# Gated delta rule: values and outputs turned in 32x32 blocks on VectorE and by transfers, gate projection token-major, another order

## The chip, the cores and the metric

One core of one Trainium2 chip runs the whole program in one launch. The metric is device time in microseconds (us) of that core, the median of several runs. The engines are TensorE (PE in the profile; PEld is its weight load), VectorE (DVE), ScalarE (ACT), GpSimd (POOL) and SyncE (SP), which here only issues transfers.

## The reference

One decoder layer in fp32 over x of 4 x 512 tokens of width 512: x plus a gated delta rule on the layernormed x, plus a retention-like cross attention with a context, plus a feed-forward with ternary weights. The change is in the first part. There are 16 key heads and 32 value heads of 128:

```
mixed = silu(causal_conv1d(h @ w_qkv, conv_w))      # taps of 4 tokens, per channel
q, k  = l2norm(q), l2norm(k);  v = v                # 16, 16 and 32 heads
beta  = sigmoid(h @ w_b);  g = -exp(A_log) * softplus(h @ w_a + dt_bias)
for each token t:                                   # per value head, state S is 128 x 128
    S = S * exp(g_t)
    S = S + k_t (x) ((v_t - k_t S) * beta_t)
    o_t = q_t S / sqrt(128)
core = o * rsqrt(mean(o^2) + eps) * norm_weight * silu(h @ w_z)
x1   = x + core @ w_out
```

## The kernel before

`head` layernorms x into xT (channels on partitions), and makes the decay tables. `delta_rule` then runs 64 units: 16 groups of heads (one key head with its two value heads) times 4 batches of 512 tokens, the batches of a group one after the other. A unit's 512 tokens are 4 chunks of 128, and within a chunk the recurrence becomes products with the inverse of a triangular matrix, found by doubling in 6 levels. `tail` does the projection with w_out and the rest of the layer.

Each engine has its own stream, written out by hand as a list of calls in one `slot` function, and the streams meet only in semaphores. A slot works on several units at once. Before the change there are three roles: `project` (unit n), `invert` (unit m = n-1) and `recur` (unit s = n-2), and `slots` runs 66 of them. The helper `long_slots`, with a fourth role `finish` (unit f = n-3) and 67 slots, is there but not used.

Names that matter, for a unit:

- `tile(n, j)` on TensorE projects one 128-wide tile over 512 tokens: k, q, v0, v1 and the gates z0, z1 (j = 0 to 5), each 4 products of 128x512 in fp32, which show as 8 instructions (L646). Each goes to one of three PSUM banks of a ring, whose order and release are written down in `RING_ORDER`, `RING_BANK` and `RING_FREED`.
- `first_tap` (ScalarE, L1116) copies a tile scaled by the last conv tap, `convolve` (VectorE, L937) adds three more, `silu` (ScalarE) finishes. The conv taps of a group lie in the last columns of `wc`, one buffer; `first_tap(n, 0)` waits for them (`taps_loaded`) in a group's first unit. SyncE reloads them after the last tap of the group's last unit, and before the change it does so in that same slot, ahead of the next slot's start.
- `k_turn`, `khat_turn`, `q_turn`, `v_turn` (L652) and `o_turn` (L803) are transposes by the identity on TensorE, four of 128x128 in a group. `copy_v` brings the turned value tile to SBUF as vn, tokens on partitions.
- `kk`, `kq` (L657): key-key and query-key products, 8 instructions. `b_full` (VectorE, L952) multiplies kk with the decay matrix, `b_high` and `b_low` split it into two fp16 parts, `e_masked`, `e_first` start the inverse.
- `level_z`, `level_d`, `level_e` (TensorE L705, L718, L730; VectorE L967, L971, L977): the doubling, a product and its follow-up on VectorE in turn; `flip_d` (L960) is VectorE's 32x32-block transpose of the fp16 matrices; for level 4 and 5 ScalarE's `copy_d` brings part of the result. `refine` and `close` (L739, L740, L747) end it with tt, the inverse.
- `solve`, `grow`, `attend`, `read_k`, `read_q` (L778, L786, L797, L758, L766): the recurrence over chunks. `solved` copies a solution to SBUF, `residual` and `next_state` (L991, L997) are VectorE's parts.
- `o_norm`, `o_scale` (GpSimd L589 to L598) normalise the output oo, `o_turn` turns it and `gated` (VectorE L1009) multiplies with the norm weight and silu(z). The result, channels on partitions, is stored to DRAM (`core_rows`), and `tail` loads it again as the weights of the output projection (L1454, four token tiles of 128 at a time, 32 heads summed).
- `load_decay(n+1)` (SyncE L472) loads the next unit's decay rows, 512 KB, broadcast to 128 partitions.
- `head_start` puts 24 early products of the output projection (L1292) between the last unit's products, so that TensorE is filled while the pipeline drains.

The lines of the taps' reload and of the wait for it:

```
if project and r % B == B - 1 and not (isinstance(g, int) and g == G - 1):
    for j in range(4):
        sp.wait_ge(projected, nth(n, "projected", j))
        load_weights(g + 1, j)
    sp.wait_ge(taps, at(n, 12, 12))
    load_weights(g + 1, TILES)
```
```
if j == 0 and r % B == 0:
    act.wait_ge(taps_loaded, (q * (ROUND // B) + r // B) * 16 + 16)
```

Of the kernel before, what the change touches and what calls it, by code (L numbers as in the profile page):

```python
# [36 lines left out]
EARLY = 24  # L37
# [70 lines left out]
def head(nc, a, xT, tabs, cons, nw, wc, w_loaded, taps_loaded):  # L108

    with ExitStack() as ctx:  # L110
# [15 lines left out]
        stats_done, mv_done, rstd_done, normed, turned, taken = (sem(n) for n in ("stats_done", "mv_done", "rstd_done", "normed", "turned", "taken"))  # L126
# [14 lines left out]
        def _(sp):  # L141
# [3 lines left out]
            for j in (0, TILES, 1, 2, 3, 5, 4):  # L145
                cols = slice(j * KT * P, (j + 1) * KT * P) if j < TILES else slice(WCOLS, GCOLS)
                sp.dma_start(wc[:, cols], a["w"][0, :, cols]).then_inc(w_loaded[j] if j < TILES else taps_loaded, 16)
# [55 lines left out]
        def _(pool):  # L203
            nc.gpsimd.memset(er[:, :, 0:1], 0.0).then_inc(starts_zeroed, 1)
            pool.wait_ge(cons_loaded, 32)
            for t in range(NT):
                pool.wait_ge(mv_done, t + 1)
# [5 lines left out]
        def _(dve):  # L213
# [8 lines left out]
            def moments(t):  # L222
                if t in PARTS:
                    dve.wait_ge(x_loaded[PARTS.index(t)], 16)
                nc.vector.bn_stats(stats[:, t, :], xs[:, t, :]).then_inc(stats_done, 1)
                dve.wait_ge(stats_done, t + 1)
                nc.vector.bn_aggr(mv[:, t, :], stats[:, t, :]).then_inc(mv_done, 1)
# [86 lines left out]
def delta_rule(nc, xT, tabs, cons, nw, wc, w_loaded, taps_loaded, acc, early, decay_dram, w_dram, core_dram, core_rows, wout):  # L314

    with ExitStack() as ctx:
# [5 lines left out]
        kraw, vraw = sb("kraw", [P, S]), [many(f"vraw{i}_", GV, [P, S]) for i in range(2)]  # L322
        khat = many("khat", 2, [P, S])
        qT, kT = many("qT", 4, [P, S]), many("kT", 4, [P, S])
        tabm = many("tabm", 4, [P, QN * GV * NC])
        ks_, vn = [many(f"ks{i}_", GV, [P, S]) for i in range(2)], [many(f"vn{i}_", GV, [P, S]) for i in range(2)]
        pT = [many(f"pT{i}_", GV, [P, S]) for i in range(2)]
        sz = [many(f"sz{i}_", GV, [P, S]) for i in range(2)]
# [6 lines left out]
        state, rr, uu, oq = sb("state", [P, GV * P]), sb("rr", [P, GV * P]), sb("uu", [P, GV * P]), sb("oq", [P, GV * P])  # L335
        oo = sb("oo", [P, GV, NC, P])
        core = sb("core", [P, NC, GV, P])
        junk, kqs = sb("junk", [P, 3 * NC, P], BF16), sb("kqs", [P, S])
# [16 lines left out]
        kq_done, p_ready, v_turned, vn_ready = sem("kq_done"), sem("p_ready"), sem("v_turned"), sem("vn_ready")  # L355
# [5 lines left out]
        or_ready, o_turned, core_ready, stored = sem("or_ready"), sem("o_turned"), sem("core_ready"), sem("stored")  # L361
# [16 lines left out]
        def nth(n, group, k, before=0):  # L378

            return at(back(n, before), len(POSITION[group]), POSITION[group][k])  # L380

# [14 lines left out]
        def by_chunk(ap):  # L396
            return ap[:, :].rearrange("p (c i) -> p c i", c=NC)

# [15 lines left out]
        def per_token(ap):  # L414
# [5 lines left out]
        RING_ORDER = ("k", "kq", "q", "k_turn", "z1", "khat_turn", "kk",  # L420
                      "v0", "q_turn", "v1_turn", "v1", "z0", "v0_turn")
        RING_BANK = {"k": 2, "kq": 0, "q": 1, "k_turn": 0, "z1": 2, "khat_turn": 2, "kk": 0, "v0": 2, "q_turn": 1, "v1_turn": 0, "v1": 0, "z0": 1, "v0_turn": 0}
# [3 lines left out]
                      "kk": (bf_ready, "bf_ready", 1), "kq": (kqs_ready, "once", 0),  # L426
                      "v0_turn": (vn_ready, "vn_ready", 0), "v1_turn": (vn_ready, "vn_ready", 1)}
        CONV_ORDER = ("k", "q", "v0", "v1")
        CONV_BUFFER = {name: i % 2 for i, name in enumerate(CONV_ORDER)}
        SILUED = {"k": (silued, "silued", 0), "q": (silued, "silued", 1), "v0": (silued, "silued", 2), "v1": (silued, "silued", 3)}  # L430
        POSITION = {"once": (1,), "squares": (1, 2, 3, 4), "projected": (1, 2, 3, 4), "tap0": (1, 2, 3, 4), "silued": (1, 2, 3, 4),
                    "taps": (1, 2, 3, 4, 5, 6, 7, 8, 9, 10, 11, 12), "e0_ready": (1, 3, 2, 4), "z_projected": (2, 1),
                    "z_silued": (2, 1), "gam_ready": (2, 1), "gamc_ready": (1, 2), "gams_ready": (2, 1), "ks_ready": (1, 2),
                    "bf_ready": (1, 2), "bh_ready": (1, 2), "bl_ready": (1, 2), "p_ready": (1, 2), "v_turned": (2, 1),
                    "vn_ready": (2, 1), "refined": (2, 1), "zr_ready": (2, 1), "closed": (1, 2), "tt_ready": (1, 2),
                    "o_turned": (1, 2), "core_ready": (1, 2)}
        RING_LAG = {"k": 0, "kq": 1, "q": 0, "k_turn": 0, "z1": 1, "khat_turn": 0, "kk": 0, "v0": 0, "q_turn": 0, "v1_turn": 1, "v1": 0, "z0": 1, "v0_turn": 1}
        CONV_LAG = {"k": 0, "q": 0, "v0": 0, "v1": 0}
# [23 lines left out]
        def _(sp):  # L462
# [13 lines left out]
            def slot(n, project, invert, recur):  # L476
                q, r = n
                g = q * (ROUND // B) + r // B
                if project and not (isinstance(q, int) and q * ROUND + r == ITERS - 1):
                    load_decay((q, r + 1))  # L480
                if project and r % B == B - 1 and not (isinstance(g, int) and g == G - 1):
                    for j in range(4):
                        sp.wait_ge(projected, nth(n, "projected", j))
                        load_weights(g + 1, j)
                    sp.wait_ge(taps, at(n, 12, 12))
                    load_weights(g + 1, TILES)
# [1551 lines left out]
```

## Time and profile before

| what | value |
|---|---|
| median of 3 runs | 3421.24 us (3419.92 to 3422.93) |
| the profiled execution's own time | 3423.98 us |
| its span, first to last instruction | 3422.1 us |
| PE busy | 3343.9 us, 98% |
| DVE busy | 2356.7 us, 69% |
| ACT busy | 1449.9 us, 42% |
| POOL busy | 1664.3 us, 49% |
| mean granted TensorE clock | 0.993 of full speed |

Shares are over the whole span, which has stages with different limits: `head` up to 70.6 us, the 64 units up to about 2600 us, `tail` after that, in which VectorE, ScalarE and GpSimd do little. A group's line number is that of the helper that issues it. A fp32 product shows as two matmul instructions. Durations of pipelined matmuls overlap, so for TensorE the distance between the starts of two groups is the better price.

### The profile page before, as it was taken

The numbers are of one execution on the slowest core, as the hardware profiler recorded it, in microseconds if no ns is written. First come the engines' busy times: TensorE is split into PE (matmuls) and PEld (weight loads), VectorE is DVE, ScalarE is ACT, GpSimd is POOL, SyncE is SP. The second block draws the span as 40 slices with busy tenths as digits, with TensorE's granted clock in tenths as the row PEclk, the third lists the DMA queues.
The fourth block names the chain that finished last, engine by engine and source line by source line (L and its number), as shares of the span: only waits on it lengthen the run. The fifth ranks groups of instructions, "written<-read, shape, count | busy, mean of one in ns | idle before, by whom it ended". The sixth has DMA issues, their size and how long they took to land. (4 is left out here: it accounts for less than half of the span.)

```text
span 3422.1 us, 57086 instructions
## 1 busy us (share of the span) xinstructions
PE 3343.9 (98%) x20832; PEld 2071.8 (61%) x20832; DVE 2356.7 (69%) x3750; ACT 1449.9 (42%) x4511; POOL 1664.3 (49%) x1630
## 2 busy tenths in 40 slices
PE   5999999999999999999999999999999999999999
PEld 2566666666666666666666666666664444454444
DVE  5788888888888888888888888888870000024453
ACT  2455555555555555555555555555540000011232
POOL 2565666666665666666665666656650000001032
PEclk8999999999999999999999999999999999999999
DMA  2021111111111111211111111111124322211001
GB/s 99 7 52 36 38 35 35 50 32 38 32 50 36 41 35 35 49 33 38 32 44 41 41 35 35 48 35 38 32 67 161 107 99 86 98 37 62 1 13 38
DMA packets 95171, 164.52 MB, mean 48 GB/s; under 512 B 7696, under 2 KB 40592, under 8 KB 93200
## 3 DMA queue, kind: packets, MB, share of 16 engines
q1 hardware_dynamic: 93600, 153.78, 15.4%
q10 hardware_dynamic: 1296, 7.08, 0.5%
q8 instruction: 171, 2.80, 0.3%
q14 instruction: 104, 0.85, 0.1%
HBM read 122.83 MB, written 38.01 MB: 47 GB/s over the span
## 5 line engine op out<-in xcount | busy, mean ns | idle before, releaser
L646 PE MATMUL acc<-xT,wc 128*128 128x512 f32 x3072 | 1403.8, 600 | 2.0 <-PEq L110 2.0
L646 PEld LDWEIGHTS acc<-xT,wc 128*128 128x128 f32 x3072 | 560.4, 191 | 560.0 <-issue 556.5
L937 DVE SCALAR_TENSOR_TENSOR d_conv<-acc,wc,d_conv 128x511 f32<-128x511 f32 (+2 forms) x768 | 569.6, 742 | 13.3 <-ACT d_conv L1116 7.3
L540 POOL TENSOR_TENSOR d_gamc<-d_gam,d_tabm 128x512 f32<-128x512 f32 x128 | 133.1, 1040 | 478.8 <-issue 462.2
L1454 PE MATMUL acc<-t_area 128*128 128x512 f32 x768 | 332.5, 592 | 1.0 <-DMA t_area<-core_rows 1.0
L960 DVE STREAM_TRANSPOSE d_em<-d_dm 128x1024 f16<-128x1024 f16 x256 | 317.3, 1239 | 4.4
L967 DVE TENSOR_TENSOR d_zm<-d_tz,cons 128x512 f16<-128x512 f32 x384 | 261.5, 681 | 77.5 <-PE d_tz L705 77.5
L1116 ACT ACTIVATE d_conv<-acc,wc 128x512 f32<-128x512 f32 x256 | 177.6, 694 | 256.0 <-PE acc L646 256.0
L1685 DVE TENSOR_TENSOR t_x<-acc,t_x 128x512 f32<-128x512 f32 x16 | 11.1, 692 | 383.6 <-PE acc L1454 383.6
L1947 POOL TENSOR_SCALAR t_veps<-t_mv 128x1 f32<-128x1 f32 x32 | 9.7, 303 | 540.3 <-DVE t_mv L1695 540.3
L971 DVE TENSOR_TENSOR d_dm<-acc,d_dm 128x512 f16<-128x512 f32 x256 | 177.0, 691 | 109.3 <-PE acc L718 109.2
L1454 PEld LDWEIGHTS acc<-t_area 128*128 128x128 f32 x768 | 144.6, 190 | 177.4 <-issue 175.5
L584 POOL TENSOR_TENSOR d_imd<-cons,d_dm 128x512 f16<-128x512 f32 x128 | 148.2, 1158 | 163.1 <-ACT d_dm L1177 163.1
L552 POOL TENSOR_TENSOR d_bl<-d_bf,d_bh 128x512 f16<-128x512 f32 x128 | 148.0, 1156 | 158.1 <-ACT d_bh L1156 158.1
L1188 ACT ACTIVATE d_uu<-d_psa 128x256 f32<-128x256 f32 x256 | 98.2, 384 | 216.3 <-PE d_psa L778 212.4
L705 PEld LDWEIGHTS d_tz<-d_dm,d_bh 128*128 128x128 f16 x3072 | 138.1, 98 | 82.1 <-issue 71.3
L1847 ACT ACTIVATE xT<-t_turn 128x512 f32<-128x512 f32 x32 | 18.2, 596 | 369.7 <-PE t_turn L1436 369.7
L797 PE MATMUL d_psb<-d_uu,d_pT 128*128 128x128 f32 x1024 | 168.7, 287 | 0.0
L718 PEld LDWEIGHTS acc<-d_zm,d_em 128*128 128x128 f16 x3072 | 132.9, 98 | 57.6 <-issue 37.8
L573 POOL TENSOR_TENSOR d_pT<-d_kqs,d_gamc 128x512 f32<-128x512 f32 x128 | 162.8, 1272 | 5.6 <-ACT d_kqs L1172 5.6
L545 POOL TENSOR_TENSOR d_gam<-d_gamc,cons 128x512 f32<-128x512 f32 x128 | 160.1, 1272 | 5.0
L705 PE MATMUL d_tz<-d_dm,d_bh 128*128 128x64 f16 x3072 | 153.1, 193 | 6.5 <-DVE d_dm L956 4.4
(228 smaller groups left out, 6808.1 us busy)
## 6 DMA issues: line engine op xcount, KB each, us to landing
d_decay<-decay_rows SPq DMA_DIRECT2D x64, 512.0 KB, 6.6
core_rows<-d_core SPq DMA_DIRECT2D x64, 512.0 KB, 3.3
t_area<-core_rows SPq DMA_DIRECT2D x30, 1024.0 KB, 5.5
wc<-in_w SPq DMA_DIRECT2D x96, 256.0 KB, 2.8
t_x<-in_x SPq DMA_DIRECT2D x4, 1024.0 KB, 9.8
t_area<-in_wout ACTq DMA_DIRECT2D x2, 2048.0 KB, 9.9
t_area<-in_ctx SPq DMA_DIRECT2D x4, 1024.0 KB, 7.7
out<-t_area SPq DMA_DIRECT2D x16, 256.0 KB, 2.0
```

The lines of the kernel that those rows point to most:

```text
L545: nc.gpsimd.tensor_tensor(by_chunk(gam[h]), by_chunk(gamc[n[1] % 2][h]), bc(cons[:, C_LT:C_LT + P], NC), ALU.mult).then_inc(gams_ready, 1)
L573: nc.gpsimd.tensor_tensor(pT[m[1] % 2][h][:, :], kqs[:, :], gamc[m[1] % 2][h][:, :], ALU.mult).then_inc(p_ready, 1)
L584: nc.gpsimd.tensor_tensor(half_of(imd, 5)[:, :, 0, :], bc(cons[:, C_ID + (1 - side) * HALF:C_ID + (2 - side) * HALF], GV * NC), half_of(dm ...
L646: last = nc.tensor.matmul(bank(TILE[j])[:, :], wtile(j, k), xT[:, k, r % B * S:(r % B + 1) * S], start=k == 0, stop=k == KT - 1)
L705: last = nc.tensor.matmul(packed(tz, l, (h * NC + c) * HALF, HALF), chunk(bh[m[1] % 2][h], c), even(dm, l, (h * NC + c) * P, P), start=Tru ...
L797: last = nc.tensor.matmul(chunk(psb, h), chunk(pT[s[1] % 2][h], c), chunk(uu, h), start=True, stop=True)
L937: nc.vector.scalar_tensor_tensor(c[:, d:S], bank(TILE[j])[:, 0:S - d], tap(j, KS - 1 - d), c[:, d:S], ALU.mult, ALU.add).then_inc(taps, 1)
L960: nc.vector.transpose(em[m[1] % 2][:, :], dm[:, :]).then_inc(flipped, 1)
L967: nc.vector.tensor_tensor(even(zm[l], l), packed(tz, l), bc(mask, GV * NC), ALU.mult).then_inc(z_ready, 1)
L971: nc.vector.tensor_tensor(even(dm, l), packed(td, l), even(dm, l), ALU.add).then_inc(d_added, 1)
L1116: nc.scalar.activation(conv_of(TILE[j])[:, :], bank(TILE[j])[:, :], ACT.Copy, scale=tap(j, KS - 1)).then_inc(tap0, 1)
L1454: return nc.tensor.matmul(acc[t][:, :], core[(grp * CHUNKS + q - 2) % 3][:, t, h * P:(h + 1) * P], rhs, start=head == 0, stop=head == HV - 1)
```

## The change

Values: instead of TensorE transposes and ScalarE copies, VectorE transposes the two value tiles of a unit in 32x32 blocks (`flip_v`), four transfers store the result to a DRAM scratch (`v_rows`) and one loads it back with the blocks in place, as vn.

Outputs: ScalarE scales oo (`o_scale`, 8 instructions), GpSimd multiplies it with silu(z) (`o_gate`), VectorE transposes it in 32x32 blocks (`flip_o`), and four transfers store it to `core_rows`. The norm weight no longer stands in `gated`, which is gone; it is multiplied into w_out instead, on ScalarE in `tail` and on GpSimd for the eight early heads (`weigh`). The layout in `core_rows` has the eight (head, chunk) pairs innermost, so that `tail` reads each 128x128 weight tile with 32 bytes between elements.

Gates: `z_tile` makes silu(z)'s input with tokens on partitions: 8 products of 128x256 a tile instead of 4 of 128x512.

Order: all streams run `long_slots`, and the order in each slot is another. Both gate tiles of a unit are in its third slot, one near the start and one near the end. `b_full` moves to GpSimd, after a ScalarE copy of kk (`copy_kk`). The order of tiles is k, q, v1, v0. On SyncE the reload of a group's taps moves to the next slot, behind `load_decay`. In `head` and `tail` two semaphores of the layernorm become one.

```diff
-EARLY = 24
+EARLY, SPREAD = 24, 16
-            def slot(n, project, invert, recur):        # SyncE
-                if project and r % B == B - 1 and ...:
-                    for j in range(4): ...
-                    sp.wait_ge(taps, at(n, 12, 12))
-                    load_weights(g + 1, TILES)
+            def slot(n, project, invert, recur, finish):
+                if n[0] * ROUND + n[1] < ITERS - 1:
+                    load_decay((n[0], n[1] + 1))
+                if invert:
+                    next_weights(back(n, 1), TILES)
+                if project:
+                    next_weights(n, 0)
...
+                if recur:
+                    early_load(back(n, 2))
+                if finish:
+                    store_o(back(n, 3))
+                if invert:
+                    store_v(back(n, 1))
+                if invert:
+                    load_v(back(n, 1))
+            def store_v(m):
+                sp.wait_ge(v_flipped, count(m))
+                wait(sp, v_moved, at(back(m, 1), 80, 80))
+                for a in range(NC):
+                    sp.dma_start(v_dram[m[1] % 2].rearrange("b i a n -> a i b n")[a],
+                                 vb[a * 32:(a + 1) * 32].rearrange("p b c j -> p b (c j)")).then_inc(v_moved, 16)
+            def load_v(m):
+                sp.wait_ge(v_moved, at(m, 80, 64))
+                wait(sp, r_ready, at(back(m, 2), 6, 6))
+                sp.dma_start(vn[m[1] % 2]...).then_inc(v_moved, 16)
+            def o_gate(s, h):                            # GpSimd
+                nc.gpsimd.tensor_tensor(o, o, sz[s[1] % 2][:, :, h * P:(h + 1) * P], ALU.mult).then_inc(gated, 1)
+            def z_tile(m, j):                            # TensorE
...
+                for i in range(2):
+                    for k in range(KT):
+                        last = nc.tensor.matmul(bank(f"z{j}")[:, i * GV * P:(i + 1) * GV * P]...,
+                                                xT[:, k, ...], wz[:, k, :, :], start=k == 0, stop=k == KT - 1)
-            def v_turn(m, h): ...
-            def o_turn(s, h): ...
+            def slot(n, project, invert, recur, finish): # TensorE
+                    kk(m); read_k(f, 1); level_z(s, 3); z_tile(s, 0); solve(f, 1); level_d(s, 3)
+                    tile(n, 0); level_z(s, 4); kq(s); read_q(f, 1); grow(f, 1); level_d(s, 4); level_e(s, 4)
+                    tile(n, 1); level_z(s, 5); attend(f, 1); read_k(f, 2); k_turn(n); level_d(s, 5); level_e(s, 5)
+                    read_q(f, 2); solve(f, 2); refine(s, 0); refine(s, 1); grow(f, 2); tile(n, 3); close(s, 1)
+                    read_k(f, 3); attend(f, 2); close(s, 0); level_z(m, 0); khat_turn(n); read_q(f, 3); solve(f, 3)
+                    level_d(m, 0); tile(n, 2); level_z(m, 1); solve(s, 0); attend(f, 3); level_d(m, 1)
+                    z_tile(s, 1); level_z(m, 2); q_turn(n); grow(s, 0); attend(s, 0); level_d(m, 2)
+            def flip_v(m):                               # VectorE
+                nc.vector.transpose(vb[:, :, :, :], vraw[:, :, :].rearrange("p h (c b j) -> p b (h c) j", c=NC, b=NC))
+            def flip_o(s):
+                nc.vector.transpose(ob[:, :, :, :].rearrange("p a j c -> p a c j"), oo[:, :, :, :].rearrange(...))
+            # VectorE's slot: starts convolve(m,2,3), flip_d(s,3), level_z(s,4), convolve(n,0,1), next_state(f,1,1),
+            # level_e(s,4), convolve(n,0,2), next_state(f,1,0), convolve(n,0,3), decays(n,0), level_z(s,5), output(f,1);
+            # ends flip_o(f), convolve(n,2,2), level_d(m,3), flip_v(m)
+            # ScalarE's slot: starts z_silu(s,0), b_high(m,0), solved(f,1), o_square(f,0,1), silu(m,3), first_tap(n,0),
+            # copy_kq(s), read_q(f,1,0), copy_d(s,4,1), b_high(m,1), read_q(f,1,1), silu(m,2), copy_d(s,4,0), silu(n,0)
-    core = xT[:, t, (1 - head // 4) * S + head % 4 * P:(1 - head // 4) * S + (head % 4 + 1) * P]
+    core = xT[:, head // GV, 0:2 * S].rearrange("p (n c) -> p n c", c=GV * NC)[:, :, head % GV * NC + t]
+            def weigh(part):                             # ScalarE in tail
+                act.wait_ge(w_loaded[part], 16)
+                for head in range(PARTS[part], PARTS[part + 1]):
+                    nc.scalar.activation(w[:, head, :], w[:, head, :], ACT.Copy, scale=nw[:, 0:1]).then_inc(w_weighed, 1)
```

The slots are cut here to their order of calls; each call still stands under the condition of its role.

## Rows read from the trace of the kernel before

**Rows 1.** Windows view, a stretch of the loop: busy time (instructions) of each engine, clock.

```profile
core 0: us, PE busy (x) PEld busy (x) DVE busy (x) ACT busy (x) POOL busy (x), PEclk, DMA share, GB/s
800.00:1300.00 500.00, 500.00 (x3683) 336.11 (x3682) 427.10 (x675) 266.71 (x869) 316.99 (x299) 1.00 0.15 40
```

**Rows 2.** Timeline of TensorE in one slot: start, us, what, count, idle before in brackets.

```profile
1003.76 0.61 PE L778 MATMUL d_psa<-d_rr,d_tt 128*128 128x128 f32 x4
1004.20 1.06 PE L657 MATMUL acc<-d_kT 128*128 128x128 f32 x8
1005.10 0.61 PE L786 MATMUL d_psa<-d_uu,d_ks 128*128 128x128 f32 x4
1005.54 0.40 PE L718 MATMUL acc<-d_zm,d_em 128*128 128x64 f16 x8
1005.78 3.68 PE L646 MATMUL acc<-xT,wc 128*128 128x512 f32 x8
1009.29 0.40 PE L705 MATMUL d_tz<-d_dm,d_bh 128*128 128x64 f16 x8
...
1023.24 0.61 PE L652 MATMUL acc<-cons,d_vraw 128*128 128x128 f32 x4
1023.68 3.60 PE L646 MATMUL acc<-xT,wc 128*128 128x512 f32 x8
```

**Rows 3.** Timeline of TensorE: third slot's start, 37 slots on, the drain, the tail's first product.

```profile
136.64 3.60 PE L646 MATMUL acc<-xT,wc 128*128 128x512 f32 x8
...
2450.64 3.60 PE L646 MATMUL acc<-xT,wc 128*128 128x512 f32 x8
...
2530.24 0.41 PE L705 MATMUL d_tz<-d_dm,d_bh 128*128 128x64 f16 x8 [2.31 <-DVE d_dm L956]
2530.49 0.92 PE L778 MATMUL d_psa<-d_vn,d_tt 128*128 128x128 f32 x4
...
2607.53 0.70 PE L1454 MATMUL acc<-t_area 128*128 128x512 f32 x1 [1.01 <-DMA t_area<-core_rows]
```

**Rows 4.** Groups by line and form, 1000 to 1500 us: busy us, mean ns, idle before.

```profile
L960 DVE STREAM_TRANSPOSE d_em<-d_dm 128x1024 f16<-128x1024 f16 x52 | 64.4, 1239 | 0.9
L967 DVE TENSOR_TENSOR d_zm<-d_tz,cons 128x512 f16<-128x512 f32 x78 | 53.1, 681 | 15.5 <-PE d_tz L705 15.5
L937 DVE SCALAR_TENSOR_TENSOR d_conv<-acc,wc,d_conv 128x511 f32<-128x511 f32 x51 | 37.9, 744 | 0.2
L1116 ACT ACTIVATE d_conv<-acc,wc 128x512 f32<-128x512 f32 x52 | 36.1, 694 | 51.3 <-PE acc L646 51.3
L573 POOL TENSOR_TENSOR d_pT<-d_kqs,d_gamc 128x512 f32<-128x512 f32 x26 | 33.1, 1272 | 0.0
L946 DVE TENSOR_TENSOR_SCAN d_gam<-d_decay,d_ident 128x512 f32<-128x512 f32 x26 | 31.9, 1228 | 0.0
L997 DVE SCALAR_TENSOR_TENSOR d_state<-d_state,d_tabm,d_psa 128x128 f32<-128x128 f32 x52 | 15.7, 322 | 0.0
L803 PE MATMUL d_psa<-cons,d_oo 128*128 128x128 f32 x52 | 7.9, 274 | 0.0
```

**Rows 5.** The page's DMA issues: size of each, median us from issue to landing.

```profile
d_decay<-decay_rows SPq DMA_DIRECT2D x64, 512.0 KB, 6.6
core_rows<-d_core SPq DMA_DIRECT2D x64, 512.0 KB, 3.3
```

**Rows 6.** Timeline of SyncE's queue, one issue of decay rows.

```profile
1101.90 0.51 SPq L472 DMA_DIRECT2D d_decay<-decay_rows  x1
```

**Rows 7.** The weight loads' line, one issue: duration ns, start; us to landing.

```profile
L466 SPq DMA_DIRECT2D wc<-in_w x1: 346/346/346, 1104.4 to 1104.4; - x1
...
DMA to landing us min/median/max: 5.1/5.1/5.1
```

**Rows 8.** DMA view, 1137 to 1140.3 us: the reload of the conv taps.

```profile
wc<-in_w SPq DMA_DIRECT2D x1, 8.0 KB, 1.7
```

**Rows 9.** Windows view of 1 us behind idle time of TensorE, columns as in rows 1.

```profile
105.00:106.00 1.00, 0.61 (x9) 0.62 (x10) 0.99 (x2) 0.00 (x0) 0.00 (x0) 0.50 0.00 0
```

**Rows 10.** The page's group of the weight loads of the output projection.

```profile
L1454 PEld LDWEIGHTS acc<-t_area 128*128 128x128 f32 x768 | 144.6, 190 | 177.4 <-issue 175.5
```

More of the change, by code:

```diff
@@ L378, in nth @@
         def nth(n, group, k, before=0):
-            return at(back(n, before), len(POSITION[group]), POSITION[group][k])
+            place = POSITION[group][k]
+            if isinstance(place, int):
+                return at(back(n, before), len(POSITION[group]), place)
+            u = at(back(n, before), 1, 1)
+            return sum(min(max(u + d, 0), ITERS) for d in place) if u > 0 else 0
         def wtile(j, k):
@@ new lines, in store_o @@
+            def store_o(s):
+                g, b = s[0] * (ROUND // B) + s[1] // B, s[1] % B
+                sp.wait_ge(o_flipped, count(s))
+                rows = core_dram[b, :, g, :, :].rearrange("(a i) q n -> q i a n", i=32)
+                for q in range(NC):
+                    sp.dma_start(rows[q], ob[q * 32:(q + 1) * 32].rearrange("p a j c -> p a (j c)")).then_inc(stored, 16)
+            for u in range(ITERS):
+                slot((u // ROUND, u % ROUND), True, u >= 1, u >= 2, u >= 3)
@@ L820, in slot @@
                 if project:
                     tile(n, 0)
+                if recur:
+                    level_z(s, 4)
+                    kq(s)
+                if finish:
+                    read_q(f, 1)
+                    head_start(f, 4)
+                    grow(f, 1)
+                    head_start(f, 5)
+                if recur:
+                    level_d(s, 4)
+                    level_e(s, 4)
+                if project:
+                    tile(n, 1)
+                if recur:
+                    level_z(s, 5)
@@ new lines, in slot @@
+                if finish:
+                    attend(f, 1)
+                    head_start(f, 6)
+                    read_k(f, 2)
+                    head_start(f, 7)
+                if project:
+                    k_turn(n)
+                if recur:
+                    level_d(s, 5)
+                    level_e(s, 5)
+                if finish:
+                    read_q(f, 2)
+                    head_start(f, 8)
+                    solve(f, 2)
+                    head_start(f, 9)
@@ L1014, in slot @@
                 if invert:
                     flip_e0(m)
+                if recur:
+                    close(s, 1)
+                if finish:
+                    residual(f, 3, 1)
+                    output(f, 2)
+                    residual(f, 3, 0)
+                if invert:
+                    level_z(m, 0)
+                if recur:
+                    close(s, 0)
+                if invert:
+                    level_d(m, 0)
+                    flip_d(m, 0)
                 if project:
@@ L1108, in _ @@
+            long_slots(dve, slot)
         @block.scalar
```

745 lines of the change are left out of this document (376 added, 369 removed).

## The prediction

> **What bounds the kernel now.** Read first the windows view over the loop: in 500 us TensorE is busy for 500, VectorE for 427, ScalarE 267, GpSimd 317, at clock 1.00 [rows 1]. The span is set by TensorE's own work there. The timeline of TensorE says the same: each group starts as the one before has issued, with no bracketed idle, and slots repeat after (2450.64 - 1023.68)/37 = 38.57 us [rows 2, 3]. So a group's price is the distance between starts: a turn of four transposes 0.44 (1023.24 to 1023.68), a projection tile 3.51, eight 128-column products 0.90, a level's eight fp16 products 0.24, a solve or grow 0.44 [rows 2]. Anything taken off VectorE, ScalarE or GpSimd is worth nothing as long as it isn't late; anything taken off TensorE counts once per unit, 64 times.
>
> **TensorE's work.** Gone from each unit are the two value turns and two output turns, 16 transposes. L803's have the mean, 274 ns, of the same kind [rows 4], so 4 x 0.44 = 1.76 us, and 64 x 1.76 = 113 us. The gate tiles change from 8 instructions of 512 columns to 16 of 256. A 512-column one takes 3.51/8 = 0.44, a 128-column one 0.90/8 = 0.11 [rows 2]: time goes by columns, weight loads are hidden even behind 128. So 16 x 0.22 = 3.5, as before. The bound is zero on one side and, if 0.02 is lost per instruction, 0.6 us a unit on the other; I take zero. A full slot becomes 36.8 us.
>
> **The other engines.** VectorE loses two products from PSUM (0.68 each, as L967's) and two gatings (a scalar_tensor_tensor of 512, as the tap's 0.74) and gains two 32x32 flips of 128x1024. Only the fp16 flip is in the trace, 1.24 [rows 4]. Change per unit: -2.84 + 2.48 = -0.4 if fp32 costs the same, +2.1 if it costs double. 427/500 of 38.57 is 32.9 us, so 32.5 to 35.0 of 36.8: not the bound, but thin at the upper end. I take 1.24. [...] ScalarE trades two value copies for one kk copy and eight small scalings, about +2 on 20.6 us; GpSimd trades one 1024-wide scaling for four 512-wide products like p_full's 1.27 [rows 4], about +3 on 24.4. Both stay far under 36.8 [rows 1].
>
> I laid the new order out as running sums, time zero at a slot's kk. VectorE ends each slot blocked on level_d(m, 3), since TensorE issues that product in the next slot, behind kk, a read, a level and a gate tile: 0.9+0.4+0.2+3.5+0.4 = 5.5, done 5.8. Then level_d 0.6, flip_v 1.2, the last v0 tap. From there each product meets its input. The thinnest places are two-step level links, 1.2 us apart where a VectorE product of 0.68 and two hand-overs of about 0.2 (estimate) must fit. I allow 0.1 us a slot, +5 in all.
>
> **A transfer that is late, once per group.** SyncE's queue is where I find a new stall. There is one buffer of conv taps; its reload, for a group's first unit, stands behind load_decay, and that behind the previous slot's store_o, store_v and load_v. In slot time:
> flip_v ends at 5.8 + 0.2 + 0.6 + 1.2 = 7.8. Four store_v issues at about 0.4 each start by 9.0. Their data follow store_o's 512 KB; a 512 KB store lands 3.3 after issue [rows 5] and 8 KB 1.7 [rows 8], so the last 128 KB lands about 2.3 after its issue, 11.3. load_v waits for exactly that. It issues at 11.4, load_decay at 11.9, the taps at 12.4. A decay load half a microsecond behind another 512 KB lands after 6.6, its median [rows 5], here at 18.3. A load issued behind a decay load lands after it: decay issued at 1101.90, weights at 1104.44, which took 5.1 where 8 KB alone takes 1.7 [rows 6 to 8]. The taps land at T = 18.8. The range for T: 13.9 if they pass the queue (12.2 + 1.7), 20.5 if store_v, from 32 partitions at a time, takes a microsecond more.
>
> first_tap(n, 0) would be due at 9.5, when the k tile ends. It is in ScalarE's queue ahead of both copy_d(s, 4), which TensorE's level_z(s, 5) waits for, and conv(n, 0, 1) on VectorE waits for it ahead of level_e(s, 4) and level_z(s, 5). TensorE runs on to 15.3 and stops. After T: the k tap 0.7; on VectorE three taps, two state updates, level_e, the scan and level_z: 3 x 0.66 + 2 x 0.28 + 0.6 + 1.16 + 0.6 = 4.9 (starts are about 0.08 under the means [rows 4]); hand-over 0.1. So level_d(s, 5) goes at T + 5.7. By TensorE's sum it was due at 16.9 (kk 0.9, three tiles 10.5, kq 0.9, six levels 1.4, seven groups of 0.45). Delay T - 11.2 = 7.6 us, nothing later makes it good because TensorE is the bound. Idling has a second price: after 2.31 us without work a solve takes 0.92 where 0.61 is usual [rows 2, 3], and the granted clock is 0.50, the lower of its two levels (1.2 of 2.4 GHz) [rows 9]. Some 4 to 7 us of work at half clock follow such pauses, a loss of 2 to 3.5, part of it under the wait: +2.1. Together 9.7 a group, 15 groups: +146 us. With T at 13.9 it is 2.7 + 1.5, +63.
>
> The Trainium skill ("DMA: Bandwidth & Descriptors", Queues, rings and completion order) has each engine consume a queue's descriptors in ring order, which is what rows 6 and 7 look like; without it, the taps would come at 13.9.
>
> **Ends.** Today the last full slot ends at 136.64 + 62 x 38.57 = 2528 and the tail's products start at 2607.5 [rows 3]: 80 us for two part-filled slots and the hand-over. After, each end has three part-filled slots and 61 are full; summing the chains, filled and drained parts come out even to about 10 us, of either sign. The longer drain leaves more waits; the fill interleaves better. Scaling w_out on ScalarE delays the tail's first product by about 3.5 (behind the second core load, then one 0.6 copy), within that allowance. I take 0. The early loads, weigh on GpSimd (4 to 5 us each) and the last store fit under the early products.
>
> **Sum.** 3424.0 (the profiled execution's own time) - 113 + 146 + 5 + 0 = 3462; the median of runs is 2.7 lower, so 3459.
>
> **Rivals.** *The taps pass the queue or the chain is shorter* (T near 14): 3424 - 113 + 63 + 5 - 3 = 3376, faster. For it: the loads are tiny. Against: rows 6 and 7. *No boundary stall at all*: 3424 - 113 + 5 - 3 = 3313, faster; it decides if T is below 11.2, for which load_v would have to issue as soon as store_v does. Against it stands the code's wait; for it, that I may have one engine's phase wrong by several microseconds. *The two nearly cancel*: at 7.5 us a group, 113, the time is 3424 + 5 - 3, no change. *Every slot stalls too*: flips in fp32 at double price put flip_v at 9 and VectorE late for level_d(s, 4) by about 1 us; 61 slots add 61: 3520. Against: same element count as the fp16 flip.
> *Weight loads at a stride.* In the tail each core tile is now read as weights with 32 bytes between elements. A load takes 0.19 and hides behind a 0.44 product [rows 2, 10]; it decides when the load is over 2.3 times dearer. At three times, 0.57 - 0.44 = 0.13 on 832 loads is +108: 3567. No row has such a load. The Trainium skill ("Advanced Engine Details and Errata", SBUF Cachelines) warns that each access to a new 16-byte line pays a penalty; this pattern is of that kind, and the page gives no size.
>
> **Chances.** Forecast 0.45 (own range 3430 to 3490); short queue 0.12; no stall 0.18; cancelling 0.08; every slot 0.12; strided weights 0.05. 0.2% (7 us) is about what a measurement can tell here. Faster 0.34 (0.30 and the forecast's low end), same 0.09, slower 0.57. The range 3310 to 3525 leaves out the strided weights, the lower half of the no-stall case and the upper tail of the stall in every slot.
>
> **What would show it.** A slot between boundaries of 36.8 us without TensorE idle; no transposes of values or outputs; every fourth slot ScalarE waiting some 9 us ahead of first_tap's k, TensorE idle for about 7 ahead of level_z(s, 5) and clock 0.5 after it; landing of the 8 KB taps 6 us or more instead of 1.7. I am wrong if every fourth slot is as long as the others (then SyncE's chain is shorter than I count), if fp32 flips take over 2 us, or if L1454's successor shows weight loads over 0.44.

## The result, and the profile after

The changed kernel takes 3459.78 us (median of 4 runs, 3454.11 to 3462.62), the kernel before 3420.69 in the same session: a ratio of 1.0111 with a 95% interval of 1.0094 to 1.0129, so 1.1% slower. Its profiled execution took 3462.62 us with a span of 3460.8; before, 3423.98 and 3422.1.

The page of the changed kernel: busy time of each engine, and the groups that answer to the change or to its stall (mean ns of one behind the busy us, then idle time before and its releaser).

```profile
span 3460.8 us, 58766 instructions
...
PE 3280.4 (95%) x20832; PEld 2322.3 (67%) x20832; DVE 2408.3 (70%) x3622; ACT 1548.4 (45%) x4983; POOL 1860.7 (54%) x1824
...
L1010 DVE SCALAR_TENSOR_TENSOR d_conv<-acc,wc,d_conv 128x511 f32<-128x511 f32 (+2 forms) x768 | 561.8, 731 | 128.1 <-ACT d_conv L1185 127.4
...
L1546 PEld LDWEIGHTS acc<-t_area 128*128 128x128 f32 x768 | 239.4, 314 | 87.1 <-issue 2.1
...
L1185 ACT ACTIVATE d_conv<-acc,wc 128x512 f32<-128x512 f32 x256 | 174.2, 681 | 194.2 <-DMA wc<-in_w 133.1
L790 PE MATMUL d_tz<-d_dm,d_bh 128*128 128x64 f16 x3072 | 156.8, 195 | 106.0 <-ACT d_dm L1254 99.7
...
L1019 DVE TENSOR_TENSOR_SCAN d_gam<-d_decay,d_ident 128x512 f32<-128x512 f32 x128 | 201.9, 1577 | 0.0
...
L597 POOL TENSOR_TENSOR d_bl<-d_bf,d_bh 128x512 f16<-128x512 f32 x128 | 191.3, 1494 | 0.0
```

One chain of three lines carries the stall: ScalarE's first_tap (L1185) waits 133 us in all for a DMA into wc, VectorE's convolve (L1010) waits 127 for first_tap, and TensorE's level_z (L790) waits 100 for ScalarE's copy_d (L1254), which stands behind first_tap in ScalarE's queue, the second of the two by seven instructions. The waits view says how often.

```profile
ACT d_conv L1185 <- DMA wc<-in_w: 133.1, 15, 10.0
DVE d_conv L1010 <- ACT d_conv L1185: 127.4, 19, 9.1
...
PE d_tz L790 <- ACT d_dm L1254: 99.7, 17, 7.5
```

Fifteen times 8.9 us: the number of group boundaries. One boundary slot on TensorE, columns as in [rows 2]; a slot runs from one `acc<-d_kT` to the next.

```profile
968.01 1.14 PE L747 MATMUL acc<-d_kT 128*128 128x128 f32 x8
...
990.89 0.61 PE L790 MATMUL d_tz<-d_dm,d_bh 128*128 128x64 f16 x8 [7.28 <-ACT d_dm L1254]
991.31 1.20 PE L883 MATMUL d_psb<-d_uu,d_pT 128*128 128x128 f32 x4
992.31 1.06 PE L843 MATMUL d_psa<-d_state,d_kT 128*128 128x256 f32 x2
993.16 1.06 PE L742 MATMUL acc<-cons,d_kraw 128*128 128x128 f32 x4
...
1014.82 0.91 PE L747 MATMUL acc<-d_kT 128*128 128x128 f32 x6
```

It is 46.81 us long, one of the longer of the 15 (45.3 to 46.9). The ordinary slots around it are 36.86 without idle time, where the slot before the change was 38.57 [rows 3]. Behind the idle time groups of four products take 1.06 and 1.20 instead of 0.60: the windows view of the same place has the granted clock (last columns: clock, DMA share, GB/s).

```profile
988.00:990.00 2.00, 0.00 (x0) 0.50 0.00 0
990.00:992.00 2.00, 1.11 (x11) 0.50 0.00 0
992.00:994.00 2.00, 2.00 (x9) 0.50 0.00 0
994.00:996.00 2.00, 2.00 (x21) 0.50 0.00 0
996.00:998.00 2.00, 2.00 (x26) 0.97 0.02 4
```

SyncE's queue, ScalarE and VectorE in that slot, from their timelines: the stores of outputs and values, load_v, load_decay, the taps, and who waited.

```profile
974.36 1.77 SPq L552 DMA_DIRECT2D core_rows<-d_ob  x4
976.62 1.75 SPq L538 DMA_DIRECT2D v_rows<-d_vb  x4
980.18 0.34 SPq L544 DMA_DIRECT2D d_vn<-v_rows  x1
980.56 1.52 SPq L480 DMA_DIRECT2D d_decay<-decay_rows  x1
982.12 0.47 SPq L474 DMA_DIRECT2D wc<-in_w  x1
```
```profile
987.04 0.69 ACT L1185 ACTIVATE d_conv<-acc,wc 128x512 f32<-128x512 f32 x1 [9.72 <-DMA wc<-in_w]
...
990.46 0.38 ACT L1254 ACTIVATE d_dm<-acc 32x256 f16<-32x256 f32 x1
```
```profile
987.76 0.75 DVE L1010 SCALAR_TENSOR_TENSOR d_conv<-acc,wc,d_conv 128x511 f32<-128x511 f32 x1 [8.81 <-ACT d_conv L1185]
...
990.85 2.11 DVE L1019 TENSOR_TENSOR_SCAN d_gam<-d_decay,d_ident 128x512 f32<-128x512 f32 x1
992.88 0.66 DVE L1045 TENSOR_TENSOR d_zm<-d_tz,cons 128x512 f16<-128x512 f32 x1
```

TensorE's product starts at 990.89, when copy_d ends. VectorE, on its own way from first_tap, ends its level_z(s, 5) at 993.54, and TensorE's level_d(s, 5), which needs that, starts at 994.01. Both links matter below.

Where the 38.7 us between the two spans went, from the starts of successive slots: over the last 61 slots of the loop, 61 x 1.712 = 104.4 us were gained, 138.6 were lost in 15 boundary slots (9.24 each, 8.4 to 10.1), and 5.0 in 15 slots two after a boundary slot (0.34 each, at most 1.3). That is +39.2; beginning, drain and tail together give -0.5.

### The profile page after: what moved, and what is told of

It is laid out like the page before. It is cut to its first block and busy times, and to the rows that moved or that the text cites. A ratio compares the mean times of both kernels' runs of the same rounds, so it can differ in the third digit from the quotient of the medians.

```text
span 3460.8 us, 58766 instructions
## 1 busy us (share of the span) xinstructions
PE 3280.4 (95%) x20832; PEld 2322.3 (67%) x20832; DVE 2408.3 (70%) x3622; ACT 1548.4 (45%) x4983; POOL 1860.7 (54%) x1824
## 5 line engine op out<-in xcount | busy, mean ns | idle before, releaser
L722 PE MATMUL acc<-xT,wc 128*128 128x512 f32 x2048 | 936.2, 600 | 2.9 <-PEq L110 2.0
L1010 DVE SCALAR_TENSOR_TENSOR d_conv<-acc,wc,d_conv 128x511 f32<-128x511 f32 (+2 forms) x768 | 561.8, 731 | 128.1 <-ACT d_conv L1185 127.4
L722 PEld LDWEIGHTS acc<-xT,wc 128*128 128x128 f32 x2048 | 369.4, 190 | 372.2 <-issue 371.0
L735 PE MATMUL acc<-wc,xT 128*128 128x256 f32 x2048 | 474.0, 384 | 2.9 <-issue 2.4
L735 PEld LDWEIGHTS acc<-wc,xT 128*128 128x128 f32 x2048 | 379.7, 190 | 50.6 <-issue 3.6
L790 PEld LDWEIGHTS d_tz<-d_dm,d_bh 128*128 128x128 f16 x3072 | 141.1, 99 | 236.7 <-ACT d_dm L1254 112.4
L1546 PEld LDWEIGHTS acc<-t_area 128*128 128x128 f32 x768 | 239.4, 314 | 87.1 <-issue 2.1
L1781 DVE TENSOR_TENSOR t_x<-acc,t_x 128x512 f32<-128x512 f32 x16 | 11.1, 692 | 389.1 <-PE acc L1546 389.1
L1284 ACT ACTIVATE d_junk<-d_oo 128x128 bf16<-128x128 f32 x512 | 158.2, 311 | 264.1 <-DVE d_oo L1081 264.1
L1185 ACT ACTIVATE d_conv<-acc,wc 128x512 f32<-128x512 f32 x256 | 174.2, 681 | 194.2 <-DMA wc<-in_w 133.1
L790 PE MATMUL d_tz<-d_dm,d_bh 128*128 128x64 f16 x3072 | 156.8, 195 | 106.0 <-ACT d_dm L1254 99.7
L1258 ACT ACTIVATE d_oq<-d_psb,d_tabm 128x128 f32<-128x128 f32 x384 | 142.6, 372 | 212.2 <-PE d_psb L851 209.5
L653 POOL TENSOR_TENSOR d_oo<-d_oo,d_sz 128x512 f32<-128x512 f32 x128 | 160.1, 1273 | 86.6 <-ACT d_oo L1237 86.6
L1019 DVE TENSOR_TENSOR_SCAN d_gam<-d_decay,d_ident 128x512 f32<-128x512 f32 x128 | 201.9, 1577 | 0.0
L1049 DVE TENSOR_TENSOR d_dm<-acc,d_dm 128x512 f16<-128x512 f32 x256 | 175.5, 685 | 33.8 <-PE acc L803 33.6
L597 POOL TENSOR_TENSOR d_bl<-d_bf,d_bh 128x512 f16<-128x512 f32 x128 | 191.3, 1494 | 0.0
## 6 DMA issues: line engine op xcount, KB each, us to landing
t_area<-in_wout ACTq DMA_DIRECT2D x2, 2048.0 KB, 13.3
```

What stands on the lines that cost most here:

```text
L597: nc.gpsimd.tensor_tensor(bl[i2][h][:, :], bf[h][:, :], bh[i2][h][:, :], ALU.subtract).then_inc(bl_ready, 1)
L722: last = nc.tensor.matmul(bank(TILE[j])[:, :], wtile(j, k), xT[:, k, r % B * S:(r % B + 1) * S], start=k == 0, stop=k == KT - 1)
L735: last = nc.tensor.matmul(bank(f"z{j}")[:, i * GV * P:(i + 1) * GV * P].rearrange("p (h n) -> p h n", h=GV), xT[:, k, r % B * S + (2 * j + ...
L790: last = nc.tensor.matmul(packed(tz, l, (h * NC + c) * HALF, HALF), chunk(bh[m[1] % 2][h], c), even(dm, l, (h * NC + c) * P, P), start=Tru ...
L1010: nc.vector.scalar_tensor_tensor(c[:, d:S], bank(TILE[j])[:, 0:S - d], tap(j, KS - 1 - d), c[:, d:S], ALU.mult, ALU.add).then_inc(taps, 1)
L1019: nc.vector.tensor_tensor_scan(gam[h][:, :], decay[r % 2][:, h, :], ident[:, :], 0.0, ALU.mult, ALU.add).then_inc(gam_ready, 1)
```

## The experiments

All start from the changed kernel but e4. Times are medians; the kernel before took 3421 to 3422 us beside them.

**e1, two sets of tap columns.** The next group's taps are loaded a slot ahead into other columns of wc; nothing else changes.

```diff
-            return wc[:, WCOLS + j * KS + k:WCOLS + j * KS + k + 1]
+            first_ = WCOLS + (n[0] * ROUND + n[1]) // B % 2 * 4 * KS + j * KS + k
+            return wc[:, first_:first_ + 1]
...
-                if invert:
-                    next_weights(back(n, 1), TILES)
+                if project:
+                    next_weights(n, TILES)
...
-                        sp.wait_ge(taps, at(n, 12, 12))
+                        wait(sp, taps, at(back(n, B), 12, 12))
```

> The changed kernel, with two sets of tap columns, so that the next group's taps are loaded a whole slot ahead, during the last unit of the group before. Theory (the taps that land 19.0 us into the slot after a group boundary cost 9.6 us at each of 15 boundaries): every slot takes 36.85 us, no boundary slot is longer, and the time is 3459.8 - 144 = about 3316 us, some 105 us under the kernel before. Rival (the new order or the VectorE turns slow every slot, and the tap wait only covers a stall that another engine would end): the wait on the taps goes and the time stays above 3420 us, with the idle time of TensorE put down to another engine.

Measured: 3325.11 us, ratio to before 0.972 (0.9706 to 0.9735). The slot that begins at a boundary, from its start to the next, on TensorE's timeline:

```profile
923.46 0.80 PE L749 MATMUL acc<-d_kT 128*128 128x128 f32 x5
...
960.31 1.14 PE L749 MATMUL acc<-d_kT 128*128 128x128 f32 x8
```

36.85 us, as all others but those two slots on, which keep their 0.34. ScalarE's idle time ahead of first_tap is now 74.5 us, all of it spent waiting for TensorE's product. The stall is the reload's alone. The rest of the change is worth 97 us. The time is 9 us over the expected 3316: the stall was taken as 9.6 us at each boundary, for taps at 19.0 us, where the means are 9.24 and 18.2, and the medians of the two kernels differ by 135 us, not 144.

**e2, e3: the same reload at two other places of SyncE's queue.** e2 puts it between load_v and load_decay:

```diff
             def slot(n, project, invert, recur, finish):
+                if invert:
+                    next_weights(back(n, 1), TILES)
                 if n[0] * ROUND + n[1] < ITERS - 1:
                     load_decay((n[0], n[1] + 1))
-                if invert:
-                    next_weights(back(n, 1), TILES)
```

> The changed kernel with the taps' reload issued ahead of load_decay instead of behind it, still behind the stores and load_v of the slot. Theory (place in SyncE's queue sets when the taps land): they land about 16 us into the slot instead of 19.0; TensorE waits about 3 us less at each of 15 boundaries, so about 3459.8 - 15 x 2.7 = 3420 us. Rival (what the taps wait for is not the queue but their last readers or the traffic): no change, 3460 us.

e3 puts it ahead of store_v, behind store_o:

```diff
-                if invert:
-                    next_weights(back(n, 1), TILES)
...
+                if project:
+                    next_weights(n, TILES)
                 if invert:
                     store_v(back(n, 1))
```

> The changed kernel with the taps' reload issued at the end of the previous slot, ahead of all stores and loads of the boundary slot. Theory: the taps land about 10.5 us into the slot, when the first tap would be taken at about 9.3 to 11.2, so the stall of TensorE is gone or under 0.5 us at each boundary: 3316 to 3325 us. Rival (one microsecond of lateness of the first tap goes straight to TensorE): 15 x 1 us more and a half clock behind it, 3340 us or above.

Measured: e2 3423.22 us, 1.0005 (0.9996 to 1.0015); e3 3326.80, 0.9723 (0.9707 to 0.9739). The timelines of SyncE in one boundary slot, e2 and then e3:

```profile
969.65 0.34 SPq L544 DMA_DIRECT2D d_vn<-v_rows  x1
970.04 1.13 SPq L474 DMA_DIRECT2D wc<-in_w  x1
971.21 0.43 SPq L480 DMA_DIRECT2D d_decay<-decay_rows  x1
```
```profile
932.21 1.78 SPq L552 DMA_DIRECT2D core_rows<-d_ob  x4
935.11 0.35 SPq L474 DMA_DIRECT2D wc<-in_w  x1
935.55 1.82 SPq L538 DMA_DIRECT2D v_rows<-d_vb  x4
```

In e2 first_tap ran at 974.24, 16.76 us into its slot (which began at 957.48), and TensorE waited 5.01. In e3 it ran at 936.84, 10.97 into its slot, after 1.67 us of waiting, and TensorE did not wait. Over the 15 boundaries of each kernel, in us, T being the time from the slot's start to that of first_tap:

| kernel | reload issued at, mean | landed after | T, mean (range) | TensorE idle | boundary slot longer by |
|---|---|---|---|---|---|
| changed | 13.3 | 4.8 | 18.2 (17.6 to 19.3) | 6.43 | 9.24 |
| e2 | 12.6 | 3.7 | 16.3 (15.8 to 17.4) | 4.54 | 6.57 |
| e3 | 9.2 | 1.7 | 11.0 (10.9 to 11.1) | 0 | 0 |

The reload is only 8 KB, and in e3 it lands 1.7 us after its issue. Behind other transfers it lands with them: in the changed kernel 0.16 to 0.20 us behind the 512 KB of decay rows at every boundary, in e2 0.17 to 0.22 us behind load_v's 512 KB at 13 of 15.

In every boundary slot of the changed kernel and of e2, TensorE's idle time is T - 11.75: 7.28 at 19.03, 5.01 at 16.76, 4.07 at 15.82. In e1, where the taps never wait, first_tap starts at 9.62, so the taps may be 2.1 us late, and from 11.75 on each microsecond goes through one to one.

Behind the idle time another 2.8 us are lost (in e2 2.0), and this is not the clock's price alone. 0.16 us belong to the wait: in an undisturbed slot the product starts that much before its predecessor's recorded end. The rest goes at clock 0.50. But VectorE's level_z(s, 5) ends 6.5 us after T in all these slots, and level_d(s, 5), due at 17.07 in e1, can't start before. Where e2's TensorE got there first, the product started at T + 6.56. So even at full clock a boundary slot would be some T - 10.5 longer, 7.7 us in the changed kernel, and the clock's own share is about 1.6 (both estimates).

**e4, the kernel before with late taps.** The one edit moves its reload behind the next slot's load_decay.

```diff
-                    sp.wait_ge(taps, at(n, 12, 12))
-                    load_weights(g + 1, TILES)
...
                     load_decay((q, r + 1))
+                if project and r % B == 0 and ...:
+                    sp.wait_ge(taps, at(back(n, 1), 12, 12))
+                    load_weights(g, TILES)
```

> The kernel before, with one step moved: the taps' reload goes behind load_decay of the slot at the group boundary. Theory (late taps alone cost what the changed kernel loses, whatever the turns are): about 6 us at each of 15 boundaries (4.2 of waiting and 2 at half clock), about 3510 us. Rival (only the changed kernel's order, with both gate products in the third slot, makes the taps critical): no change, 3421 us.

Measured: 3508.62 us, 1.0256 (1.0241 to 1.0272). Its waits view and one boundary on TensorE's timeline:

```profile
ACT d_conv L1117 <- DMA wc<-in_w: 103.2, 15, 7.2
```
```profile
1021.40 1.23 PE L787 MATMUL d_psa<-d_uu,d_ks 128*128 128x128 f32 x4 [2.96 <-ACT d_uu L1189]
```

Fifteen boundary slots are 6.06 us longer (3.20 idle on average, the rest behind it, where the clock is 0.50), all others stay at 38.57. With none of the turns' changes, this one moved line costs 87 us; it isn't particular to the new order. The expected sum of 6 was made of 4.2 of waiting and 2 behind it, so its parts were off.

**e5, sixteen transposes given back.** e1, plus 16 transposes of 128x128 in each unit ahead of the q turn.

```diff
+                for _ in range(4):
+                    for c in range(NC):
+                        nc.tensor.transpose(chunk(bank("q_turn"), c), chunk(qT[third(n)], c), cons[:, C_ID:C_ID + P])
                 turn(bank("q_turn"), qT[third(n)], q_turned)
```

> The kernel with two sets of tap columns, and 16 more 128x128 transposes on TensorE in each unit, beside the q turn (as many as the change takes away; what they write is overwritten). Theory (without the tap wait TensorE alone sets the slot, and the four turn groups that the change removes were worth 4 x 0.44 us): the slot goes from 36.86 to 38.6 us and the time from 3325 to about 3325 + 64 x 1.76 = 3438 us. Rival (another engine's chain, VectorE's 33.8 us in a slot above all, bounds the slot already): under 3380 us.

Measured: 3430.49 us, 1.0025 (1.0015 to 1.0035). Each slot is 38.61, 1.755 longer than 36.855: TensorE's work is the slot. The group of the added products, 1000 to 1500 us (13 units):

```profile
L767 PE MATMUL acc<-cons,d_qT 128*128 128x128 f32 x208 | 25.3, 275 | 0.0
```

The 0.34 us of every fourth slot vanish here (see e8), which is most of why the total is 8 under expectation. And 1.755 is 0.04 more than the change took off a slot, 1.712: the two gate tiles, in 16 products each, take 3.53 us from start to start where 3.51 was usual.

**e6, flip_o with dense output.** e1, with flip_o writing its elements in a row.

```diff
-                nc.vector.transpose(ob[:, :, :, :].rearrange("p a j c -> p a c j"), oo...)
+                nc.vector.transpose(ob[:, :, :, :].rearrange("p a j c -> p a (j c)").rearrange("p a (c j) -> p a c j", ...), oo...)
```

> The kernel with two sets of tap columns, but flip_o writes its elements in a row instead of 32 bytes apart; the stored outputs are then in a wrong order, which changes no amount of work. Theory (the 2.06 us of flip_o come from the distance between the elements that it writes, and VectorE has time to spare): the instruction takes 1.22 us as flip_v does, and the time stays at 3325 us, within 2 us. Rival (the time comes from the fp32 read pattern or from GpSimd beside it): the instruction stays at 2.06 us.

Measured: 3323.90 us, against e1's 3325.11: no difference that counts. The groups by form, of e7 (below; each flip twice) and then of e6:

```profile
L1034 DVE STREAM_TRANSPOSE d_ob<-d_oo 128x1024 f32<-128x1024 f32 x64 | 131.7, 2058 | 68.2 <-POOL d_oo L655 68.2
...
L1027 DVE STREAM_TRANSPOSE d_vb<-d_vraw 128x1024 f32<-128x1024 f32 x64 | 77.8, 1216 | 0.0
```
```profile
L1032 DVE STREAM_TRANSPOSE d_ob<-d_oo 128x1024 f32<-128x1024 f32 x64 | 79.7, 1245 | 68.2 <-POOL d_oo L655 68.2
```

With the same read pattern and the same GpSimd work beside it, 2.06 us became 1.25. The 32 bytes between the elements that flip_o writes cost 0.8 us. The fp32 type costs nothing: 1.22 and 1.25 us, where the fp16 flip took 1.24 [rows 4]. TensorE's slots are 36.86 either way.

**e7, e9, e10: the flips twice.** e1 with flip_v and flip_o each done twice in a row (e7), flip_v alone (e9), flip_o alone (e10); the second waits for the first. The edit, for flip_v:

```diff
                 nc.vector.transpose(vb[:, :, :, :], vraw...).then_inc(v_flipped, 1)
+                dve.wait_ge(v_flipped, at(m, 2, 1))
+                nc.vector.transpose(vb[:, :, :, :], vraw...).then_inc(v_flipped, 1)
```

> The kernel with two sets of tap columns, with flip_v and flip_o each done twice in a row, which adds 3.3 us to VectorE's 33.8 us in a slot of 36.86. Theory (VectorE is second in line with a margin of 3.0 us a slot, and its chains tolerate little of that at one place): VectorE becomes the bound, its work of 37.1 us a slot alone gives 3325 + 61 x 0.3 = 3343 us, and waits between engines on top may bring it to 3400 us. Rival (VectorE is so far off the path that its work can grow by a tenth): no change, 3325 us.

Measured: 3578.69 us, 1.0457 (1.0441 to 1.0472), far over both expectations. Slots are 39.8 to 41.5 long.

```profile
1142.77 0.41 PE L805 MATMUL acc<-d_zm,d_em 128*128 128x64 f16 x8 [2.51 <-DVE d_zm L1051]
```

That is level_d(s, 4), waiting for the level_z product of VectorE behind the flips. e9 and e10 were made to find how much room there is at that place.

> The kernel with two sets of tap columns, with flip_v alone done twice, 1.25 us more work for VectorE in a slot. With both flips twice (3.3 us more) TensorE waited 2.5 us for level_z at the place behind the flips. Theory (what counts is the room at that place, 3.3 - 2.5 = 0.8 us, not VectorE's idle time over the slot): TensorE waits 0.4 to 0.5 us a slot, 3325 + 61 x 0.5 = about 3355 us. Rival (only VectorE's sum counts, 35.0 of 36.86 us): no change, 3325 us.

> The kernel with two sets of tap columns, with flip_o alone done twice, 2.06 us more work for VectorE in a slot. Theory (room of 0.8 us at that place): TensorE waits 1.2 to 1.3 us a slot, and with some microseconds at half clock in part of the slots the time is 3325 + 61 x 1.3 = 3404 us or up to 3440. Rival (only VectorE's sum counts, 35.9 of 36.86 us): no change, 3325 us.

Measured: e9 3385.16 us, 0.9893 (0.9876 to 0.9909), e10 3427.75, 1.0018 (1.0008 to 1.0027). The same product on TensorE in e9 and in e10:

```profile
1107.34 0.41 PE L805 MATMUL acc<-d_zm,d_em 128*128 128x64 f16 x8 [0.65 <-DVE d_zm L1049]
```
```profile
1119.99 0.41 PE L805 MATMUL acc<-d_zm,d_em 128*128 128x64 f16 x8 [1.23 <-DVE d_zm L1049]
```

Slots are 37.86 and 38.48: 1.25 us more of VectorE's work cost 1.00, and 2.06 us cost 1.63. The rival, that only VectorE's sum counts (33.8 of 36.86 us in a slot of e1), is refuted by both. But e9 came 30 us over the expectation, and e10 24 over its first figure (under the 3440).

The expected waits were about right, 0.62 and 1.23 us, but a bracket isn't the whole delay, since in e1 the same product starts before its predecessor's recorded end, and in e10 the level_z before it is 0.2 us late already. By starts, level_d(s, 4) comes at 11.46 us into a slot of e1, 12.27 of e9, 13.08 of e10 and 14.36 of e7: 0.81, 1.62 and 2.90 late for 1.25, 2.06 and 3.3 us of work. The room at that place is 0.4 us, half of the 0.8 read from the bracket. In e9 another 0.2 us are lost on the way to level_d(s, 5).

e7 costs more than the sum of the two, 4.2 us a slot against 2.7. In 45 of its last 61 slots TensorE falls to the lower clock for a while:

```profile
1142.00:1144.00 2.00, 1.24 (x17) 0.83 0.75 191
1144.00:1146.00 2.00, 2.00 (x4) 0.50 0.45 84
```

The columns are TensorE's busy time, clock, DMA share and GB/s. The slots without such a stretch are 39.9 long, 3.1 over e1's, those with one 41.1 to 41.5: waiting costs 3.1 us in every slot, the clock some 1.2 to 1.5 in three of four.

**e8, the gate weights in one load.** e1, with the two gate tiles' weights of a group loaded by one transfer.

```diff
-                cols = slice(j * KT * P, (j + 1) * KT * P) if j < TILES else ...
+                cols = slice(j * KT * P, (j + (2 if j == 4 else 1)) * KT * P) if j < TILES else ...
...
-                if recur:
-                    next_weights(back(n, 2), 5)
```

> The kernel with two sets of tap columns, with the two gate tiles' weights loaded by one transfer instead of two issued one after the other. Theory (of each four slots one is 0.34 us longer, because the second of the two loads is issued 1.05 us after the first and lands after the first gate product of the next slot is due): that excess goes or shrinks, 3325 - 5 = 3320 us. Rival (it is the landing of a transfer of this size, not its issue, that is late): no change, 3325 us.

Measured: 3327.48 us, 0.9722 (0.9705 to 0.9738): no change, and the slot in question is still 0.36 longer. The landing is what is late. The load cannot be issued before the second gate tile of one slot has ended, at 35.2, and is due 3.3 us later, when the first gate tile of the next slot could start (at 1.64, 38.5 from the same zero). In e8 the one load of 512 KB takes 3.45 to 3.75 us to land. In e1 the second of the two, issued 0.4 us behind the first (not 1.05, as expected), lands at 38.4 to 39.7. In all 15 cases of both kernels the gate tile starts 0.1 us after that landing, and once TensorE sat idle for 1.10 us by it. e5 agrees: its added transposes stand between the two gate tiles, the next one starts at 40.25, and nothing is lost.

```profile
1000.07 3.69 PE L737 MATMUL acc<-wc,xT 128*128 128x256 f32 x16 [1.10 <-issue]
```

## Why the prediction was right, point by point

The sum was 3462 for the profiled execution, and 3462.6 came out. The two large terms have the right cause, and that they add up to the microsecond is luck: the turns brought 8 us less and the boundaries cost 7 us less than predicted. Inside the boundary term, errors cancel once more.

- **TensorE bounds the kernel, four turns are worth 1.76 us a unit.** Right: slots of 36.86 without idle time (predicted 36.8), and e5 gives 1.755 back. The size was off: -113 was predicted, but with the 0.04 of the gate tiles, and with the ends, where fewer units are in flight and other waits decide, it came to -105 (-104.4 over 61 slots, -0.5 at the ends).
- **The taps' reload stalls each boundary.** Right in place, cause and chain: first_tap, copy_d, level_z(s, 5). Step by step, load_v was issued at 12.2 (predicted 11.4), load_decay at 12.6 (11.9), the taps at 13.3 on average (12.4). They landed 4.8 us later, not 6.4, so T is 18.2 where 18.8 was predicted. The slot shown is one of five in which the issue of load_decay took over 1 us, and has the taps at 14.1 and T at 19.0.
- **The size of the delay.** The prediction priced it by VectorE's chain to level_d(s, 5), as T - 11.2. That chain is there, but it lets the product start at T + 6.6 and not T + 5.7, as the scan takes 2.1 us beside GpSimd's work where 1.16 was counted. That gives T - 10.5, or 7.7 us. The predicted 7.6 is close by luck: T was 0.6 too late and the tolerance 0.7 too large, which cancel. The idle time that the profile brackets ahead of level_z(s, 5), 6.4 us, is another quantity: there TensorE waits for ScalarE's copy_d. The clock on top was put at 2.1 and is about 1.6. Sum 9.24 a boundary, predicted 9.7: +138.6, not +146. What e1 takes away confirms the term: 134.7 us between the medians.
- **Behind the decay load.** T falls by 1.9 when the taps go ahead of it (e2), and by 7.2 when they go ahead of the values' stores as well (e3). The long way is the round trip of the values, load_v waiting for store_v to land and then landing itself, more than the decay rows. The taps don't pass the queue here: they land just behind the 512 KB ahead of them. The rows that spoke for it in the prediction were weaker than they looked, as they set the 5.1 us of a 256 KB load, whose median in that trace is 2.8 us, against the 1.7 of 8 KB.
- **+5 for thin level links.** The total was right by luck and the cause wrong. Ordinary slots lose nothing at the links; the 5.0 us are gate weights that land late, two slots after each boundary slot (e1, e8). I hadn't looked at when those loads can be issued.
- **VectorE has room.** Right, but by little, and not for the reason given. flip_v takes 1.22 as taken from the fp16 flip; flip_o takes 2.06, which I had named as a sign of being wrong. A sum per slot (33.8 of 36.86) suggests 3 us of room; e7, e9 and e10 show 0.4 at the place of the flips. The rival "every slot stalls", with flips late for level_d(s, 4), was right about the place: e9 and e10 stall just there.
- **Flips in fp32.** The Trainium skill gives the transpose one element per cycle per lane ("Vector Engine (DVE) Microarchitecture Reference", The reshape front-end and per-opcode configuration) and names no type there. Flip_v's 1.22 and e6's 1.25 in fp32, against 1.24 in fp16, agree. It doesn't tell flip_o's 2.06.
- **Strided weight loads.** The page's group has 314 ns for one of the output projection's loads, where 190 was usual [rows 10]: 1.65 times, under the 2.3 at which it would decide. The Trainium skill's warning of a penalty for each new line ("Advanced Engine Details and Errata", SBUF Cachelines) agrees; its size here would be these 0.12 us a load, hidden behind products whose starts are 0.44 apart. No run changed the distance alone. From the tail's first product to the end it is 816.8 us, against 814.6 before.
- **Ends.** Even to 0.5 us, predicted 0 within 10. The drain is longer by 6 us (last start of a k k^T product to the tail's first product: 105.0 against 99.2), the tail by 2.3, and the beginning shorter by 8.6.

## What to carry to other kernels

A change that takes work off the bounding engine can also move transfers in the issuing engine's queue, as this one did. Write down when each small load lands in the new order, beside when its first reader is due: here 8 KB per group, moved behind other transfers, cost 139 us where 105 were gained, and 16 more columns a partition (or the line moved up) give a kernel 2.8% faster than the one before. Room on a second engine is not its idle share. It is what one place in its order lets slip before the bounding engine waits, and doing an instruction there twice measures it, if one goes by the start of the product that waits and not by its bracketed idle time.

## What the runs showed of the hardware

- **TensorE's clock after a pause.** In the changed kernel it idles for 5.8 us or more at each boundary and works for some microseconds at granted clock 0.50 behind, where 2.65 us are lost on average (about 1.6 by the clock alone, as estimated above). It is also so after 2.96 us of idle time in e4, and in 45 of the last 61 slots of e7, where each slot has a pause of about 2.45 us. Pauses of 1.23 us in every slot of e10 left it at 1.00.
- **VectorE's scan and a GpSimd product slow each other.** The means of the scan and of GpSimd's product rose from 1.23 [rows 4] and 1.16 us to 1.58 and 1.49. The timelines of the two engines in e1 show one pair that overlaps, and one scan alone:

```profile
1086.44 2.01 DVE L1021 TENSOR_TENSOR_SCAN d_gam<-d_decay,d_ident 128x512 f32<-128x512 f32 x1
...
1100.76 1.18 DVE L1021 TENSOR_TENSOR_SCAN d_gam<-d_decay,d_ident 128x512 f32<-128x512 f32 x1
```
```profile
1086.20 1.16 POOL L605 TENSOR_TENSOR d_em<-d_bh,cons 128x512 f16<-128x512 f16 x1
1087.32 2.09 POOL L599 TENSOR_TENSOR d_bl<-d_bf,d_bh 128x512 f16<-128x512 f32 x1
```

  The scan starts at 1086.44, the first GpSimd product ends at 1087.36, and 2.01 is about that 0.9 plus 1.18; the next product takes 0.93 us more than alone and outlives the scan by 1.0. Each slot has both cases: in e1 the 64 scans without a GpSimd product beside them take 1.18 us, the 64 with one 1.96 on average. That they slow each other is shown; that one waits until the other has ended is only how the times read. In ordinary slots it cost nothing, as they stayed at 36.86; in the boundary slots it lengthens VectorE's chain.
- **An issue can take longer.** In the changed kernel load_decay's issue took 0.43 us at ten of the 15 boundaries and 1.02 to 1.52 at the other five, behind the same transfers; in ordinary slots, too, it is 0.4 to 1.4. In e2, where the taps came first, theirs took 1.01 to 1.30 at five boundaries. What made it so was not separated.
